# A Mamba-2 block and an attention/expert block on one core: five steps moved at the group boundaries and at the end of a batch

## What is computed

```python
xn = layernorm(x)
# branch 1: Mamba-2 (4 heads of 64, state 64), then an MLP
h  = layernorm(xn) * w + b
z, xBC, dt = split(h @ in_proj)          # dt = softplus(. + bias)
xBC = silu(causal_conv4(xBC));  xs, B, C = split(xBC)
state = state * exp(dt * A) + (dt * xs) B^T;   y = state C + D * xs
y  = rmsnorm(y * silu(z)) @ out_proj;  x1 = xn + y
s  = x1 + mlp(layernorm(x1))
# branch 2: causal attention (16 heads of 8, q and k rms-normed), then top-2 of 4 experts
a  = softmax(mask(q k^T)) v @ wo;        x2 = xn + a
g  = silu(x2 + sum of weighted experts(rmsnorm(x2)))
out = x + s * g
```

## Time and profile before

| | |
|---|---|
| time of the kernel, median of 3 runs | 869.19 us (869.1 to 870.39) |
| profiled execution, its own time | 868.79 us |
| its span, first to last instruction | 867.1 us |
| TensorE, matmuls busy | 786.9 us (91%) |
| VectorE busy | 618.0 us (71%) |
| ScalarE busy | 499.2 us (58%) |
| GpSimd busy | 323.9 us (37%) |
| mean granted TensorE clock | 0.992 of full speed |

### The profile page before, as it was taken

The page is one execution under the profiler, slowest core; times in us unless marked ns, Lnnn a source line. Parts: engine busy times, 40 slices in busy tenths (PEclk is TensorE's granted clock), DMA queues, the critical chain, the costliest instruction groups (busy, mean ns, idle before and its releaser), DMA issues. The chain is left out here.

```text
span 867.1 us, 18101 instructions
## 1 busy us (share of the span) xinstructions
PE 786.9 (91%) x5472; PEld 481.4 (56%) x5472; DVE 618.0 (71%) x1469; ACT 499.2 (58%) x928; POOL 323.9 (37%) x600
## 2 busy tenths in 40 slices
PE   2779999998999989998999989999899998999897
PEld 1455554755556564654647555474556556474555
DVE  2776479775888768776696768877587876967634
ACT  2335784466754775457744667537765568446552
POOL 5424533153512717045340545227160362505400
PEclk9998999999999999999999999999999999999999
DMA  4000000000000000000000000000000000000000
GB/s 165 2 8 20 8 0 2 9 15 25 0 8 12 14 12 0 8 14 24 0 0 8 14 24 0 2 18 2 24 0 8 13 25 0 0 8 14 24 2 13
DMA packets 15145, 11.73 MB, mean 14 GB/s; under 512 B 1040, under 2 KB 13968, under 8 KB 14992
## 3 DMA queue, kind: packets, MB, share of 16 engines
q1 hardware_dynamic: 15120, 11.43, 4.4%
HBM read 7.76 MB, written 2.10 MB: 11 GB/s over the span
## 5 line engine op out<-in xcount | busy, mean ns | idle before, releaser
L1102 ACT ACTIVATE sb_pr<-S 128x768 f32<-128x768 f32 (+1 forms) x192 | 163.8, 879 | 135.6 <-PE S L445 135.6
L1199 DVE TENSOR_REDUCE sb_mx<-S 128x2 f32<-128x256 f32 (+3 forms) x256 | 197.7, 816 | 29.3 <-PE S L445 28.8
L1723 POOL TENSOR_SCALAR_AFFINE_SELECT sb_pr<-sb_pr 128x256 f32<-128x256 f32 (+1 forms) x192 | 99.4, 523 | 299.3 <-ACT sb_pr L1102 299.0
L445 PE MATMUL R<-sb_pr,sb_va 128*32 128x512 f32 (+3 forms) x1024 | 89.4, 444 | 9.7 <-POOL sb_pr L1723 7.6
L445 PE MATMUL R<-sb_W,sb_pr 128*128 128x96 f32 (+1 forms) x512 | 69.5, 276 | 0.0
L445 PE MATMUL R<-sb_xfT,sb_W 128*128 128x512 f32 x144 | 69.2, 602 | 0.0
L445 PE MATMUL S<-sb_kT,sb_qT 32*128 32x256 f32 (+3 forms) x512 | 56.3, 384 | 13.8 <-DVE sb_mx L1199 10.9
L1187 DVE RECIPROCAL sb_rden<-R 128x16 f32<-128x16 f32 x32 | 8.2, 258 | 83.9 <-PE R L563 53.4
L445 PEld LDWEIGHTS R<-sb_W,sb_pr 128*128 128x128 f32 x512 | 63.5, 192 | 3.8 <-issue 3.5
L445 PEld LDWEIGHTS S<-sb_kT,sb_qT 32*128 32x128 f32 x512 | 27.5, 183 | 66.4 <-DVE sb_mx L1199 58.7
L445 PE MATMUL S<-sb_qT,sb_kT 32*128 32x256 f32 (+3 forms) x512 | 56.3, 384 | 2.9 <-ACT sb_pr L1102 1.9
(11 more groups left out here) (217 smaller groups left out, 1709.0 us busy)
## 6 DMA issues: line engine op xcount, KB each, us to landing
sb_xin<-x SPq DMA_DIRECT2D x9, 256.0 KB, 2.9
sb_W<-weights SPq DMA_DIRECT2D x1, 2290.0 KB, 10.9
sb_qT<-sb_mT SPq DMA_DIRECT2D x128, 4.0 KB
sb_xres<-x SPq DMA_DIRECT2D x8, 256.0 KB, 2.8
out<-sb_xres SPq DMA_DIRECT2D x7, 256.0 KB, 2.3
sb_cT<-sb_xact SPq DMA_DIRECT2D x8, 128.0 KB, 2.3
sb_W<-weights SPq DMA_DIRECT2D x1, 514.0 KB, 5.8
sb_cst<-consts SPq DMA_DIRECT2D x1, 328.0 KB, 3.1
```

What stands on the lines that cost most here:

```text
L445: return pe.matmul(o, lhsT, rhs, start=start, stop=stop, skip_group_check=True)
L1102: act.activation(pr[:, e % 4, :, 0:n], S[pair_of_exp(e)][:, :, 0:n], ACT.Exp).then_inc(p_sb, 1)
L1199: o = dve.tensor_reduce(mx[:, n // P - 1, g, heads[0]:heads[1] + 1], found[:, :, at_col:at_col + n], AX.X, ALU.max, negate=True)
L1723: pool.affine_select(out=keep, in_=keep, compare_op=ALU.is_ge, fill=0.0, base=0, pattern=pattern, channel_multiplier=-1)\
```

## The change

Five steps change their place; nothing is computed differently.

```diff
--- before
+++ after
@@ PE stage_b
                 if tail:
 
+                    pe.wait_ge(oT_sb, at(oT_sb, r, 0))
+                    pe.wait_ge(yz_sb, at(yz_sb, r, 0))
+                    for t in range(T):
+                        i = pe.transpose(R[3][:, t * P:(t + 1) * P], oT[:, 1, t * P:(t + 1) * P], ident)
+                    i.then_inc(ot3_ps, 1)
+
                     pe.wait_ge(yT_sb, at(yT_sb, r, 0))
                     for t in range(T):
                         for n in range(2):
                             i = mm(R[2][:, t * P:(t + 1) * P], yT[:, n, t * P:(t + 1) * P],
                                    w2("op", D)[:, n, :], n == 0, n == 1)
                     i.then_inc(op_ps, 1)
-
-                    pe.wait_ge(oT_sb, at(oT_sb, r, 0))
-                    pe.wait_ge(yz_sb, at(yz_sb, r, 0))
-                    for t in range(T):
-                        i = pe.transpose(R[3][:, t * P:(t + 1) * P], oT[:, 1, t * P:(t + 1) * P], ident)
-                    i.then_inc(ot3_ps, 1)
@@ PE stage_a
                     if u == 4:
                         if g > 0:
                             weigh_values(r, e - 2)
-                        scan_outputs(r, g)
                         if g == T - 1:
                             prep_a(r)
-                        elif g > 0:
+                        scan_outputs(r, g)
+                        if 0 < g < T - 1:
                             new_state(r, g)
                     if g == 0 and u == 5:
                         new_state(r, 0)
                         weigh_values(r, 2)
+                weigh_values(r, G * UNITS - 2)
                 turn_y(r, T - 1)
-                weigh_values(r, G * UNITS - 2)
@@ ACT stage_a
                     exponentiate(r, e)
-                    if u == 0 and g > 0:
+                    if u == 1 and g > 0:
                         evac_values(r, g - 1)
-                    if u == 1 and g > 0:
                         evac_y(r, g - 1)
...
+                evac_values(r, G - 1)
                 evac_y(r, T - 1)
                 square_y(r, T - 1)
-                evac_values(r, G - 1)
@@ POOL stage_a
-                    if u == 3 and g < T - 1:
+                    if u == 5 and g < T - 1:
                         decays(r, g + 1, tail)
```

## The result

The changed kernel took **861.28 us** (median of 5 runs, 860.88 to 864.96) beside 870.39 us of the kernel before in the same comparison (median of 5, 869.10 to 871.26). The ratio is 0.9901, 95% interval 0.9886 to 0.9915: 9.1 us or 1.0% faster, where 4.6 us were forecast. The profiled execution took 861.28 us with a span of 859.5 us, against 868.79 and 867.1 of before.

What follows compares the result with a forecast made beforehand. TensorE, nearly always occupied, was taken as the bound, so gains come from its waits. Eight stages by 0.45, seven boundaries by 0.06 and 0.54 once make 4.6 us: 864.6 us, own range 862.9 to 866.2, wider range 862.0 to 867.3.

Steps and rivals of the forecast that it cites:

- Copy term: Groups 0 to 1 and 1 to 2: value-sum copy behind the second wide exponential brings weighings 0.55 us sooner per stage.
- Group 2 to 3, GpSimd sets it: GpSimd's sum ahead of unit 18's weighing stays; of the 0.55 us sooner start, 0.45 us per stage remains.
- Boundary: Stage end to next q/k/v matmuls, from the last scan outputs' start W: 6.84 instead of 6.90 us, 0.06 gained.
- Last stage: No q/k/v follow: VectorE's block on the projection's result starts at W + 7.06 instead of 7.60; 0.54 us gained once.
- The decay operand, nothing in the sum: Group 0: operand behind unit 5's mask fits ahead of the segments; no loss counted, 0.25 us in the range.
- The collision in group 0: VectorE's subtraction and first-state copy held until GpSimd's operand ends; segments lose 0.25 us if the operand takes 1.49 us.
- TensorE sets group 2 to 3 too: Rival, chance 0.12: GpSimd done half a microsecond sooner, 0.93 us per stage, 8.4 us in all, 860.8 us.
- GpSimd gives all of it back: Rival, chance 0.12: GpSimd's chain ends at 709.30 regardless; only boundaries and last stage remain, 0.94 us, 868.2 us.
- The slower rival: Chance 0.06: last weighing doesn't fit ahead of the turn of y; a boundary costs 0.73 us, 871.4 us.

Runs made afterwards that it cites:

- a2_copies_back: Changed kernel with ScalarE's copies of the value sums put back between the two wide exponentials: 868.28 us, steady batch 101.36 us against the changed kernel's 100.57.
- a3_end_back: Changed kernel with the whole end of the stage (transposes, last weighing, turn of values, ScalarE order) put back: 865.45 us, batch 100.79 us against 100.57.
- a1_operand_back: Changed kernel with the decay operand put back ahead of the masks of units 4 and 5: 860.71 us, batch 100.50 us against 100.57.
- a4_transposes_alone: Kernel before with only the next input's four transposes moved ahead of the last scan outputs: 877.59 us, ratio 1.0090, batch 101.95 us against 101.60.
- c2_norms_moved_operand_back: c1_norms_moved with the decay operand put back ahead of the masks of units 4 and 5: 863.12 us, batch 100.44 to 100.66 us against 100.01.
- c1_norms_moved: Changed kernel, transposes between last weighing and turn of y, ScalarE's end reordered, plus GpSimd's last norm step behind unit 21's mask: 859.66 us, batch 100.01 us.
- c4_norms_split: Like c1_norms_moved, but the norm step is cut: power behind unit 19's mask, short products behind unit 21's: 852.94 us, ratio 0.9801, batch 99.34 us.
- b2_projection_first: Changed kernel with the output projection again ahead of the turn of the value sums: 865.70 us, ratio 0.9940, batch 100.91 us (one distance).
- b1_weigh_first_alone: Kernel before with only the last weighing moved ahead of the turn of y, value copy ahead of y copy: 871.75 us, ratio 1.0004, batch 101.63 us.

## Why the prediction was wrong

The sign was right, and so was the engine that sets each place in the middle of the stage. The size was not: 8.8 us by the ledger where the sum had 4.6. The terms for the copies and the boundary were mis-sized, and one step of the last stage named the wrong limit.

- **Copy term, 0.55 forecast, 0.80 measured** (0.34 + 0.46; a2_copies_back 0.79). The step that failed is "TensorE's scores of unit 8 can't start before the segment matmuls end (687.87 + 1.02 = 688.89), the weighing not before 688.89 + 0.45 = 689.34". Those are durations of single rows. What follows on the same engine starts sooner: the scores 0.96 us behind the segments' start, the weighing 0.38 behind the scores. A row's duration includes a tail in which the next instruction already runs. The Trainium skill (Perfetto Trace Analysis, "Tensor Engine Instruction (MATMUL, LD_WEIGHTS)") says that a TensorE row begins with the prefetch of its operands and that its end is computed, not observed; the trace agrees in that rows reach past the next start: 1.02 us of row against 0.96 us to the next start, and 0.45 against 0.38. At group 1 to 2, where I used the start-to-start distance for the segments but the duration for the scores, the miss was half as large in proportion (0.35 forecast, 0.46 measured). Even that distance, 1.10 us, was not TensorE's own: it ended with unit 7's exponential (687.89 + 1.03 = 688.92, scores at 688.97). With the exponential early, it is 1.06 at this place.
- **Group 2 to 3, GpSimd sets it.** Right: the unit 16 wait gone, one left ahead of unit 18, GpSimd's sum passes on the gain from its start. The forecast took 0.1 us off the gain for unit 16's exponential and it was 0.04 in all (the row of work begins 0.29 us later against the turn of the values, and is 0.25 shorter). This term was small; its input, the 0.55, was the wrong one. 0.80 - 0.04 = 0.76 stands where 0.45 stood, in all eight stages: 2.5 of the 4.2 us missed.
- **Boundary, 0.06 forecast, 0.27 measured** (a3_end_back 0.22). The failed step is "four transposes 0.61, so y is 0.61 later". They put 0.38 on the y path (3.80 - 3.42), since they issue in 0.49 and the first scan matmuls behind them take 0.11 less. So y came 0.23 us sooner than forecast. The steps behind it were off as well, and it is luck that they cancel. The turn of the values follows the turn of y by 0.58 us instead of 0.37, with the loop's jump between them (0.45 in the last stage). The projection follows it by 0.46 instead of 0.55, as TensorE gets there later than the y copy ends. And q/k/v follow the projection by 1.79 instead of 1.89: here, full-width matmuls directly behind four transposes take 0.10 less than behind a weighing (rows of 1.95 against 2.05, and 0.60 against 0.70 for the first scan outputs). Seven times 0.21 is 1.5 us.
- **Last stage, 0.54 forecast, 0.86 measured.** The block on the projection's result starts at W + 6.82 instead of W + 7.06, by the same error of the transposes. Another 0.17 us is a step that was wrong in kind. The sum at 824.51 was not set by the block: in the trace of before it starts as the attention output's projection ends (823.34 + 1.13 = 824.47). It came 2.65 us behind the block's start, and now comes 2.48 behind, with the attention output out of the way. That makes 0.96 us at the sum; 0.10 of it is lost again by the last instruction.
- **The decay operand, nothing in the sum**: right (a1_operand_back). The collision in group 0 that I kept for the range came about, below, and reached nothing.
- **The range** ended at 862.0. Its bounds, 0.25 to 0.65 us per stage and 0.2 gained or lost per boundary, stood around middle values made of durations and shared their error: 0.76 and 0.27 both lie outside. The upper bound for the copies, 0.75 us, was passed by 0.05, and the range took only 0.65 for the stage, though GpSimd passes on all but 0.04.
- **The rivals.** "TensorE sets group 2 to 3 too" gave 860.8 us, near the measured 861.28, but its mechanism didn't happen: the wait for GpSimd is still there and longer (0.86 us). A near number from a rival isn't that rival. "GpSimd gives all of it back" would be a wait of about 1 us: it was 0.86, yet GpSimd's own time from the turn of group 1's values is the same as before (9.46 against 9.42 us), so what lengthened the wait is TensorE arriving sooner. The slower rival's condition, a last weighing that doesn't fit ahead of the turn of y, didn't come about: 0.65 us of waiting is left behind it (709.14). Its price for the transposes was too high as well: with nothing in the gap they cost 0.35 us a batch (a4_transposes_alone).

## What to carry to other kernels

Cost work on the engine that is the bound by start-to-start distances of rows in the same neighbourhood; durations overstate what stands in line, and here the range built from them missed on the same side. When one wait is cut, ask what the releasing engine's whole sum is until its next deadline: reordering inside that sum is worth nothing as long as the later deadline is the one that binds (a1_operand_back, and c2_norms_moved_operand_back for when it isn't), and taking a piece out of it into a later idle stretch is worth the whole wait, if that stretch is long enough for the piece (c1_norms_moved against c4_norms_split). Of parts that move together, try each alone: here one copy made three quarters of the gain, and two of the five parts (the operand, the transposes) could be left out of the changed kernel at no cost. Try each both ways, too: the transposes alone, in the kernel before, cost 0.35 us a batch.

## What the runs showed of the hardware

**Half clock for a few us.** The windows view of the changed kernel around one fall; columns: stretch, length, busy us and instructions of TensorE, its weight loads, VectorE, ScalarE and GpSimd, granted clock, DMA share, GB/s.

```profile
800.00:802.00 2.00, 1.51 (x6) 0.49 (x6) 1.47 (x5) 1.41 (x4) 1.74 (x5) 1.00 0.12 35
802.00:804.00 2.00, 1.39 (x8) 0.20 (x8) 0.64 (x2) 1.80 (x3) 1.37 (x4) 0.65 0.33 96
804.00:806.00 2.00, 2.00 (x11) 1.53 (x8) 0.34 (x2) 0.00 (x0) 0.00 (x0) 0.50 0.45 131
806.00:808.00 2.00, 2.00 (x25) 1.17 (x23) 1.66 (x5) 1.16 (x2) 0.18 (x1) 1.00 0.00 0
```

TensorE was busy 1.51 of 2 us in the stretch ahead of the fall and 1.39 in the one in which it came, with the wait of 0.86 us for unit 18's masks across both. Its clock went to the 1.2 GHz level (0.50) and came back. The weighing of unit 18 took 1.93 us there instead of 1.06. In b2_projection_first the clock falls at 631.4 us, behind three waits of 0.93, 0.32 and 0.34 us. A batch with a fall is 1.35 to 1.6 us longer. How many there are differs between executions of one program: the changed kernel's had mean clocks from 0.984 to 0.994. Where they lie differs less. From the second batch to the seventh, in every trace kept, a fall starts either 30 us behind the batch's first segment matmuls, where unit 18's weighing starts, or 52 to 55 us behind them, as in b2_projection_first. With the last batch counted, the first place has a fall in five of the six traces with the 0.86 us wait ahead of unit 18, and in none of the eight without it. So this wait and the falls there go together; that it causes them, no run shows by itself. a4_transposes_alone, with the longest wait ahead of y, had the low clock in four of four executions, but b1_weigh_first_alone, with the same batch as before, had 0.988 to 0.997.

**A small VectorE subtraction beside GpSimd's operand.** In group 0 of the changed kernel:

```profile
679.39 1.04 POOL L1706 TENSOR_TENSOR sb_rs<-sb_cst,sb_dta 128x512 f32<-128x512 f32 x1
679.49 0.97 DVE L1207 TENSOR_TENSOR sb_mhl<-sb_mx,sb_mhl 128x16 f32<-128x16 f32 x1
```

16 columns took 0.97 us where they took 0.18, and they end with the operand (679.39 + 1.04 = 680.43, 679.49 + 0.97 = 680.46). This is the held instruction that the prediction described; the segments at 681.32 don't feel it. By the rule of the Trainium skill cited there (SBUF — State Buffer, "Who interferes with whom") the one that issues second is held for the whole of the other. Here the trace agrees: VectorE's issued 0.10 us later and ended with GpSimd's. In group 2 to 3 the first join shrank from 1.52 us to 1.12, the two masks from 2.13 to 1.84, and the power grew from 1.63 in before's order (a1_operand_back) to 1.89; GpSimd's row of work is 6.79 us instead of 7.04. That the collisions moved and their sum hardly changed is how I read it; no run takes the joins away.
